# GpSimd takes four of the eight score comparisons of each head in chunks 1 to 3 of a two-layer graph attention kernel

## The reference, cut to what matters

```python
Wh = (h @ W).reshape(N, H, D)
e = s_src[:, None, :] + s_dst[None, :, :]      # one score per pair of nodes and head
e = where(e >= 0, e, 0.2 * e)
e = where(adj[:, :, None] > 0, e, -9e15)
attention = softmax(e, axis=1)
h_prime = einsum('ijh,jhd->ihd', attention, Wh)
```

## Time and profile before

| | |
|---|---|
| median of 3 runs | 917.73 us (917.41 to 917.98) |
| profiled execution, first to last instruction (span) | 916.2 us |
| TensorE (PE) matmuls busy | 841.2 us, 92% |
| VectorE (DVE) busy | 765.8 us, 84% |
| ScalarE (ACT) busy | 691.3 us, 75% |
| GpSimd (POOL) busy | 43.0 us, 5% |
| mean granted clock of TensorE | 0.974 of full |

### The profile page before, as it was taken

How to read it: one execution, slowest core, us unless ns; L and a number is a source line. 1 busy time by engine, 2 the same in 40 slices (tenths; PEclk the granted TensorE clock), 3 DMA queues, 4 the chain that set the end, 5 groups by cost and what they waited for, 6 DMA issues and landing times.

```text
span 916.2 us, 24392 instructions
## 1 busy us (share of the span) xinstructions
PE 841.2 (92%) x10868; PEld 689.3 (75%) x10868; DVE 765.8 (84%) x1334; ACT 691.3 (75%) x810; POOL 43.0 (5%) x80
## 2 busy tenths in 40 slices
PE   8687999989999889999998897699999999999993
PEld 6686999979999889999998884355555555555551
DVE  3979889899988999889997889775877787777787
ACT  3999898898999989999977994958264563738202
POOL 3200000000000000000000000000000000000000
PEclk9899999999999999999999899799999999999997
DMA  8999377704659128023040011430335344353200
GB/s 146 176 105 247 52 75 90 231 25 40 80 71 222 58 25 94 26 94 126 16 117 25 1 42 53 70 104 13 108 96 165 97 160 143 130 180 97 70 12 14
DMA packets 41921, 84.67 MB, mean 92 GB/s; under 512 B 6226, under 2 KB 31188, under 8 KB 41172
## 3 DMA queue, kind: packets, MB, share of 16 engines
q0 software_dynamic: 12416, 33.56, 26.2%
q1 hardware_dynamic: 29396, 49.50, 15.2%
HBM read 112.27 MB, written 21.12 MB: 146 GB/s over the span
## 4 chain that ended last, share of the span: by engine, by line
PE 60%; ACT 19%; DVE 17%; issue 3%; DMA 0%; SPq 0%; DVEq 0%; ACTq 0%
PE bank L1212 28%; PE bank L634 21%; ACT ring L566 14%; PE bank L1199 7%; DVE ring L599 3%; DVE ring L579 3%; PE bank L482 2%; ACT masks L469 2%; ACT moving L519 1%; DVE ring L603 1%; DVE ring L609 1%; DVE evac L650 1%; ACT masks L489 1%; PE bank L1150 1%; PE bank L1140 1%
## 5 line engine op out<-in xcount | busy, mean ns | idle before, releaser
L634 PE MATMUL bank<-moving,ring 128*128 128x99 bf16 (+1 forms) x6528 | 452.5, 218 | 12.0 <-DVE ring L609 8.8
L634 PEld LDWEIGHTS bank<-moving,ring 128*128 128x128 fp8e4 x6528 | 388.3, 98 | 14.3 <-DVE ring L609 10.0
L566 ACT ACTIVATE ring<-s_rows,scores 128x1024 fp8e4<-128x1024 f32 x372 | 393.4, 1143 | 3.5 <-PE bank L634 2.7
L634 PE MATMUL bank<-moving,masks 128*128 128x99 bf16 x1664 | 223.1, 209 | 18.0 <-DVE evac L650 14.9
L1212 PE MATMUL bank<-moving,masks 128*128 128x387 bf16 x1152 | 194.4, 327 | 0.0
L634 PEld LDWEIGHTS bank<-moving,masks 128*128 128x128 fp8e4 x1664 | 163.3, 98 | 19.8 <-DVE ring L603 8.3
L1212 PEld LDWEIGHTS bank<-moving,masks 128*128 128x128 fp8e4 x1152 | 111.0, 96 | 79.6
L713 ACT ACTIVATE masks<-s_rows,adj_tiles 128x512 fp8e4<-128x512 f32 x256 | 157.8, 709 | 0.1
L356 ACT ACTIVATE ring<-ring 128x4 f32<-128x4 f32 (+1 forms) x27 | 5.5, 205 | 158.6 <-DVE ring L312 124.2
L599 DVE SCALAR_TENSOR_TENSOR ring<-ring,masks 128x1024 int32<-128x1024 int32 x93 | 113.1, 1217 | 10.9 <-ACT ring L566 10.8
L609 DVE TENSOR_TENSOR ring<-masks,ring 128x1024 int32<-128x1024 int32 x76 | 93.1, 1225 | 26.9 <-PE bank L634 25.1
(11 more groups left out here) (186 smaller groups left out, 599.3 us busy)
## 6 DMA issues: line engine op xcount, KB each, us to landing
masks_kept<-masks SPq DMA_DIRECT2D x4, 4096.0 KB, 16.8
masks<-masks_kept SPq DMA_DIRECT2D x8, 2048.0 KB, 9.7
adj_tiles<-in_adj_dram POOLq DMA_DIRECT2D x24, 512.0 KB, 8.2
s_rows<-score_rows SPq DMA_DIRECT2D x14, 512.0 KB, 4.8
ring<-masks_kept POOLq DMA_DIRECT2D x11, 512.0 KB, 3.9
first_part<-masks_kept POOLq DMA_DIRECT2D x11, 512.0 KB, 4.7
second_part<-masks_kept POOLq DMA_DIRECT2D x10, 512.0 KB, 3.8
adj_tiles<-in_adj_dram POOLq DMA_DIRECT2D x16, 256.0 KB, 15.4
```

The costliest lines, as they stand in the source:

```text
L566: last = act.activation(j_tile(below, k), s_rows[:, h % 2, :], ACT.Sign, bias=scores[:, g * JU + k, h:h + 1], saturate=False)
L634: last = pe.matmul(bank[b][:, at + lo:at + hi], mask, moving[:, j, h, lo:hi], start=first, stop=(j == T - 1), skip_group_check=True)
```

## The change

Three things. In chunks 1 to 3 the units with even g are compared by GpSimd, those with odd g by ScalarE, none by VectorE (before: six of eight by ScalarE and two by VectorE; seven and one in the last head). GpSimd computes (s_i + d_j) * -1e20 in one `tensor_scalar` of two operations and lets the conversion to a byte saturate; VectorE then ands with the masks and with 0x40 in one `scalar_tensor_tensor`. The table `DIRECT` has 4 D units each in chunks 1 and 2 (before 8 each) and 12 in chunk 3 (before 19). GpSimd's loads of the adjacency move into the stream of its comparisons: after the comparison of unit u stand the loads that wait for the groups which TensorE turns in front of unit u. Chunk 0 stays as it is.

```diff
+FAR = -1e20
-    ON_ACT = [... "AVAVAAVA"
-              "AVAAVAAA" "AVAAVAAA" "AVAAVAAA" "AVAAVAAA"
...
-              "AVAAVAAA" "AVAAVAAA" "AVAAVAAA" "AAAAVAAA"]
+    COMPARES = ("VAVAAVAA" "AVAVAAVA" "AVAVAAVA" "AVAVAAVA"
+                "PAPAPAPA" "PAPAPAPA" "PAPAPAPA" "PAPAPAPA"
...
+    ON_ACT, ON_DVE, ON_POOL = ([who == one for who in COMPARES] for one in "AVP")
     DIRECT = [how == "D" for how in
               "DDDDDDDD" "DD-D----" "DD-D----" "DD-D----"
-              "DD------" "DD------" "DD------" "DD------"
-              "DD------" "DD------" "DD------" "DD------"
-              "DD-DD-D-" "DD-DD-D-" "DD-DD-D-" "DD-D-D--"]
+              "D-------" "D-------" "D-------" "D-------"
+              "D-------" "D-------" "D-------" "D-------"
+              "DD-D----" "DD-D----" "DD-D----" "DD-D----"]
...
+        def pool_unit(pool, c, u):
+            h, g = divmod(u, UH)
+            if g == 0:
+                wait_s(pool, c, u)
+            if ON_POOL[c * U + u]:
+                wait_slot(pool, c, u)
+                below = below_slot(c, u).bitcast(U8)
+                for k in range(JU):
+                    last = pool.tensor_scalar(j_tile(below, k), s_rows[:, h % 2, :], scores[:, g * JU + k, h:h + 1],
+                                              FAR, ALU.add, ALU.mult)
+                last.then_inc(pool_compared, 1)
+            if g == UH - 1:
+                pool.wait_ge(pool_compared, pool_count(c, u + 1))
+                pool.sem_inc(s_read_pool, 1)
...
+            elif ON_POOL[c * U + u]:
+                dve.wait_ge(pool_compared, pool_count(c, u + 1))
+                dve.scalar_tensor_tensor(out=below, in0=below, scalar=TWO * 0x01010101, in1=m, op0=ALU.bitwise_and,
+                                         op1=ALU.bitwise_and).then_inc(done, 1)
...
                     sp.wait_ge(s_read_dve, before)
+                    if before > H:
+                        sp.wait_ge(s_read_pool, before - H)
...
+                def load_next(c, t):
+                    if c == 1 and t < AHEAD:
+                        pool.wait_ge(turned, (QUARTERS - 1 + t // 2) * (Q // QUARTERS))
+                    else:
+                        pool.wait_ge(turned, c * Q + (t - AHEAD + 1) * QT)
+                    load_adj(pool, c, t)
+                for t in range(CT):
+                    load_next(1, t)
+                for t in range(AHEAD):
+                    load_next(2, t)
                 for c in range(1, NC):
-                    for t in range(CT):
...
-                        load_adj(pool, c, t)
+                    for u in range(U):
+                        pool_unit(pool, c, u)
+                        for q in groups_at(c, u):
+                            t = q // QT
+                            if q % QT == QT - 1 and t + AHEAD < CT:
+                                load_next(c + 1, t + AHEAD)
+                            elif q % QT == QT - 1 and c + 2 < NC:
+                                load_next(c + 2, t + AHEAD - CT)
```

More of the change, by code:

```diff
@@ L88, in two_layer_gat @@
     W0 = 2 * PARTS * K0
-    ON_ACT = [who == "A" for who in
-              "VAVAAVAA" "AVAVAAVA" "AVAVAAVA" "AVAVAAVA"
-              "AVAAVAAA" "AVAAVAAA" "AVAAVAAA" "AVAAVAAA"
-              "AVAAVAAA" "AVAAVAAA" "AVAAVAAA" "AVAAVAAA"
-              "AVAAVAAA" "AVAAVAAA" "AVAAVAAA" "AAAAVAAA"]
+    COMPARES = ("VAVAAVAA" "AVAVAAVA" "AVAVAAVA" "AVAVAAVA"
+                "PAPAPAPA" "PAPAPAPA" "PAPAPAPA" "PAPAPAPA"
+                "PAPAPAPA" "PAPAPAPA" "PAPAPAPA" "PAPAPAPA"
+                "PAPAPAPA" "PAPAPAPA" "PAPAPAPA" "PAPAPAPA")
+    ON_ACT, ON_DVE, ON_POOL = ([who == one for who in COMPARES] for one in "AVP")
     DIRECT = [how == "D" for how in
               "DDDDDDDD" "DD-D----" "DD-D----" "DD-D----"
-              "DD------" "DD------" "DD------" "DD------"
-              "DD------" "DD------" "DD------" "DD------"
-              "DD-DD-D-" "DD-DD-D-" "DD-DD-D-" "DD-D-D--"]
+              "D-------" "D-------" "D-------" "D-------"
+              "D-------" "D-------" "D-------" "D-------"
+              "DD-D----" "DD-D----" "DD-D----" "DD-D----"]
     GQ = 8
@@ L273, in two_layer_gat @@
         s_in = sems("s_head_in0", "s_head_in1")
-        s_read_act, s_read_dve = sems("s_read_act", "s_read_dve")
+        s_read_act, s_read_dve, s_read_pool, pool_compared = sems("s_read_act", "s_read_dve", "s_read_pool", "pool_compared")
         signs_ready, compared, below_ready, unit_ready, unit_done, acc_ready, acc_taken = sems(
@@ L526, in dve_count, with pool_count @@
         def dve_count(c, u):
-            return c * U + u - act_count(c, u)
+            return sum(ON_DVE[:c * U + u])
+        def pool_count(c, u):
+            return sum(ON_POOL[:c * U + u])
         def below_slot(c, u):
@@ L586, in dve_unit @@
                 wait_s(dve, c, u)
-            compare_next = g + 1 < UH and not ON_ACT[c * U + u + 1]
+                if not any(ON_DVE[c * U + u:c * U + (h + 1) * UH]):
+                    dve.sem_inc(s_read_dve, 1)
+            compare_next = g + 1 < UH and ON_DVE[c * U + u + 1]
             if compare_next and (c > 0 or h > 0):
@@ L603, in dve_unit @@
                 dve.tensor_tensor(below, below, m, ALU.bitwise_and).then_inc(done, 1)
-                if all(ON_ACT[c * U + u + 1:c * U + (h + 1) * UH]):
+                if not any(ON_DVE[c * U + u + 1:c * U + (h + 1) * UH]):
                     dve.sem_inc(s_read_dve, 1)
@@ L1069, in _ @@
                 sp.wait_ge(s_read_dve, (NC - 1) * H + 3)
+                sp.wait_ge(s_read_pool, (NC - 2) * H + 3)
                 load_s1(sp, 0)
@@ L1107, in _ @@
                     load_quarter(pool, k)
-                for c in range(1, NC):
-                    for t in range(CT):
[L1110 to L1113, removed]
-                        load_adj(pool, c, t)
+                def load_next(c, t):
[8 more added lines that the diff above has]
+                    load_next(2, t)
+                for c in range(1, NC):
+                    for u in range(U):
[6 more added lines that the diff above has]
+                                load_next(c + 2, t + AHEAD - CT)
                 pool.wait_ge(unit_done, NC * U)
```

## The result

The changed kernel takes 1010.1 us (median of 4 runs, 1009.65 to 1011.18) against 917.9 us before: ratio 1.100, 95% interval 1.099 to 1.102. It is 10% slower. The profiled execution has a span of 1009.3 us.

A forecast was written before the change was run, and what follows sets the result against it. ScalarE was taken as the bound, with TensorE and VectorE close behind. 916.2 + 101 (full exclusion) + 8 (lost lead) = 1025, and 1.5 around the span: 1027 us; range 905 to 1100, about 8 in 10.

The forecast's parts named there:

- lost lead: GpSimd's stream, chunks 1 and 2: waits for TensorE's transposes before loads delay the next comparison; 8 us taken.
- Full exclusion: GpSimd's comparisons and VectorE's two-input instructions never overlap, so their times add in chunks 1 to 3: +101 us; chance 0.53.
- inner term: GpSimd's hold on the path shared with VectorE: 64 x (1.4 - 0.10) = 83.2 us a chunk.
- eight and four places: Units where GpSimd's lead falls to zero: eight in chunk 1, the first four in chunk 2, none in chunk 3.
- the case without exclusion: GpSimd and VectorE don't block each other: stalls add 24 us in chunk 1 and 6.5 in chunk 2.
- stall of up to 0.8 us: TensorE at even units where GpSimd waited: 8.9 us of work against TensorE's 6 to 8.5.
- The floor of 113 for chunk 3: TensorE's busy time of 108.0 us with the waits for sums in chunk 3: 113 us.
- Rival 1: Chunks 1 to 3: no exclusion, GpSimd quick, only lost lead and TensorE count; 905 us, -12.5; chance 0.17.
- the theories by waits alone: Only waits for GpSimd cost: the kernel before with the spare comparisons would take 916 to 922 us.
- Rival 2: Chunks 1 to 3: no or partial exclusion, GpSimd's instruction time as the price; middle 945 us; chance 0.26.
- the path shared by turns: Branch of Rival 2: each two-input VectorE instruction longer by 0.2 to 0.4 us, +15 to +50 us.
- The signs named: L599 and L609 over 1.22 us or GpSimd-ended idle, TensorE waiting for GpSimd units' ands, lower clock, chunk 3 slow as chunk 1.

The follow-up runs named there:

- the run with the late loads: The changed kernel with each adjacency load six units further on in GpSimd's stream: 976.0 us, ratio 1.064.
- the stage with both: Stage of a separate test kernel: 16 GpSimd comparisons and 16 VectorE ands of 128 x 1024 at once, 34.7 us.
- the spare comparisons: The kernel before plus 192 GpSimd comparisons into a tile nobody reads, adjacency loads six units later: 1024.8 us, ratio 1.116.
- the run with the spare memsets: The kernel before plus 192 GpSimd memsets of 128 x 1024 bytes that nobody waits for, adjacency loads six units later: 950.8 us, ratio 1.034.

## Why the prediction was right

1027 us was forecast with slower at 0.78, 1010 us measured. The mechanism is the forecast's: the two streams hardly overlap, and a lost lead comes on top. That the number came so near is in part luck, as below.

**Full exclusion.** Taken as 154, 154 and 160 us a chunk from 1.4 us an instruction. GpSimd's instruction is 1.19 us apart from the next. With 64 x (1.19 - 0.10) = 69.8 us in place of 83.2 the same sum gives 140, 140 and 147; the run with the late loads has 138.6, 138.2 and 147.4. So the sum comes within 2 us with one term corrected, by 0.21 us an instruction, 40 us over the three chunks. Its inner term is not shown, though. It has GpSimd hold the path for 1.09 us, and the stage with both shows VectorE stopped for 0.84; with that the same sum gives 124, 124 and 131. In chunk 1 of the run with the late loads most of the difference is VectorE's idle time, 13 us, 10 of them spent waiting for GpSimd. Whether the cast's 0.28 us has a fixed part over 0.10 no run shows. The estimate of 1.54 us from the 1.8 cycles of the Trainium skill's GPSIMD Engine Reference, § 3.1, would have been further off.

**The lost lead.** Its eight and four places were right. I took 8 us, on the argument that VectorE could use the path while GpSimd waits; it is 34. VectorE had nothing to do then: it waits 48.9 us for GpSimd in chunk 1. The 30.5 us that I had worked out for the case without exclusion (24 + 6.5) were the better figure, although their "stall of up to 0.8 us" at even u doesn't follow: against TensorE's 6 us the 8.9 leave up to 2.9. The 8 us for the lost lead are the step of the forecast that failed. The two errors, -40 and +26, hid each other, which is luck: the three chunks came to 458.5 us against 476 forecast. By stage, with all 8 us put into chunk 1, the forecast was 6 us too low in chunk 1 (162 against 167.8) and 10 and 13 too high in the others.

**What the change gives back.** ScalarE at 85 us and VectorE at 94 in chunk 1 were as worked out (84.4, and 96.0 with the comparisons left out). The floor of 113 for chunk 3 was wrong, 127.6 measured. The forecast's sum didn't rest on it, but the times of rivals 1 and 2 did.

**The rivals.** Rival 1, no exclusion, needed 1.4 us or less an instruction and had that with 1.19. It would most likely not have ended faster even so, for it counted on 114 us for chunk 3, which takes 127.6 without any comparison. By the forecast's own working the lost lead at 1.19 us an instruction is some 25 us, and on top of the 902.7 us without comparisons that makes 928, an estimate. It and the theories by waits alone fall with the spare comparisons, for which nobody waits. Rival 2's last branch, the path shared by turns, had VectorE's side right: two-input instructions longer by 0.2 to 0.4 us, where the ands and xors of chunk 1 are longer by 0.22 in the mean, and by 0.39 with the late loads. Its +15 to +50 us was too little, for the run with late loads is 58 us slower than the kernel before; it left out that GpSimd's own comparisons grow, to 2.03 us each. The signs named came out in part: xors over 1.22 us, idle time before L625 ended by GpSimd (in chunks 1 and 2), a lower granted clock. Two did not. TensorE's waits are for the xors (L635), and none is recorded for the and of a GpSimd unit. And chunk 3 is not as slow as chunk 1, because the lost lead is larger than I had it.

## What to carry to other kernels

Before work goes to an idle engine, ask what it shares: each of GpSimd's comparisons of 1.19 us could stop VectorE for some 0.8 us and itself grow to 3 us behind VectorE, and most of VectorE's time here went to two-input instructions or comparisons, which the stages above show to be stopped. If GpSimd must help, take from VectorE what meets it in the worst way (its wide comparison) and keep the share small: two of eight, with none left on VectorE, was 6 us faster than the kernel before, four of eight 58 us slower with the loads late. And when compute is put into a stream that issued transfers, the transfers' waits go with it: the lead over the slowest engine is lost at each of them, and issuing the transfers six units later gave 34 us back without any other change.

## What the runs showed of the hardware that was not expected

- VectorE and GpSimd don't take turns evenly. In the stage with both, VectorE's 16 ands were done after 24.1 us in place of 18.3, GpSimd's 16 only after 34.5. The 5.9 us more are 7 times 0.84: VectorE was stopped once for each two of its instructions, and GpSimd waited behind two of VectorE's for each of its own.
- VectorE's comparison suffers most: 10.7 us for 16 alone, 23.6 beside GpSimd's. A write-only memset holds it up as well: in the run with the spare memsets the longest of its instructions, 4.23 us against 0.75, stood still beside four memsets in a row.
- On GpSimd the same comparison written with `is_lt` and a multiply takes 3.69 us, with an add and a multiply that saturates 1.19.
